# Steps of five tiles and a block of 128 nodes, with one-hots compared into PSUM and weighted from there

## The reference

```python
def _rgcn_conv(x, src, dst, et, basis, comp, root, bias):
    W = jnp.einsum('rb,bio->rio', comp, basis)
    xw = jnp.einsum('ni,rio->nro', x, W)
    msgs = xw[src, et]
    seg = dst * N_REL + et
    summed = jax.ops.segment_sum(msgs, seg, num_segments=N_NODES * N_REL)
    cnt = jax.ops.segment_sum(jnp.ones((msgs.shape[0],), x.dtype), seg, num_segments=N_NODES * N_REL)
    mean = summed / jnp.maximum(cnt, 1.0)[:, None]
    agg = mean.reshape(N_NODES, N_REL, HIDDEN).sum(axis=1)
    return agg + x @ root + bias
...
h = x
for l in range(N_LAYERS):
    h_new = jax.nn.relu(_rgcn_conv(h, src, dst, edge_type, basis[l], comp[l], root[l], bias[l]))
    h = h_new + h
...
out = _layernorm(x + h)
```

## Time and profile before

| | us |
|---|---|
| runs shown | 5449.66, 5447.10, 5457.17; median 5449.66 |
| the profiled execution, its own time | 5442.3 |
| its span | 5440.0 |
| granted TensorE clock over the span | 0.583 of full speed |
| PE busy | 2179.6 (40%) |
| DVE busy | 1661.3 (31%) |
| ACT busy | 1425.4 (26%) |
| POOL busy | 3015.8 (55%) |

### The profile page before, as it was taken

One profiled execution on the slowest core, in us unless ns is written; L12 is line 12 of the kernel. 1 busy time (PEld: TensorE's weight loads), 2 busy tenths in 40 slices (PEclk: granted clock), 3 DMA queues, 4 the chain that ended last, 5 costly groups with the idle time before them and its releaser, 6 DMA issues. The chain is left out here.

```text
span 5440.0 us, 53285 instructions
## 1 busy us (share of the span) xinstructions
PE 2179.6 (40%) x8413; PEld 1711.0 (31%) x8413; DVE 1661.3 (31%) x4647; ACT 1425.4 (26%) x4065; POOL 3015.8 (55%) x3194
## 2 busy tenths in 40 slices
PE   7823333333333333333496133333333333333336
PEld 4412232333223223233343133223333322333336
DVE  7402233233233233323320123223333323332336
ACT  5612222222222222222254022222222222222225
POOL 0355566665666656566303666666666665656652
PEclk9956555555555555555698555555555555555557
DMA  7711111111111111111054111111111111111113
GB/s 227 273 38 41 42 45 43 44 44 41 44 44 43 43 41 44 42 44 44 24 232 172 44 44 43 43 43 44 44 44 44 43 44 41 45 42 44 43 38 95
DMA packets 180986, 337.44 MB, mean 62 GB/s; under 512 B 64632, under 2 KB 104616, under 8 KB 180932
## 3 DMA queue, kind: packets, MB, share of 16 engines
q0 software_dynamic: 101488, 209.20, 14.7%
q1 hardware_dynamic: 53472, 114.78, 5.8%
q10 hardware_dynamic: 25972, 12.87, 0.9%
HBM read 225.40 MB, written 111.23 MB: 62 GB/s over the span
## 5 line engine op out<-in xcount | busy, mean ns | idle before, releaser
L332 POOL DMA_INDIRECT ring<-products,idx x3000 | 2830.1, 943 | 2037.9 <-issue 924.5
L713 PE MATMUL bank<-onehot,rows 128*128 128x128 f32 x6656 | 1668.7, 431 | 3086.5 <-DVE onehot L878 2439.6
L713 PEld LDWEIGHTS bank<-onehot,rows 128*128 128x128 f32 x6656 | 1438.6, 319 | 3316.8 <-DVE onehot L878 2467.4
L548 ACT ACTIVATE rows<-ring,relnorm 128x128 f32 x3328 | 1051.8, 389 | 3681.2 <-remote 2237.7
L888 DVE TENSOR_TENSOR aggT<-aggT,bank 128x128 f32 x3328 | 951.8, 286 | 1914.9 <-issue 1389.0
L878 DVE TENSOR_TENSOR onehot<-bank,relnorm 128x512 f32<-128x512 f32 x832 | 573.1, 689 | 1609.6 <-issue 1551.4
L623 PE MATMUL bank<-W,hT 128*128 128x512 f32 (+1 forms) x784 | 344.3, 598 | 12.5 <-ACT ring L503 7.2
L503 ACT ACTIVATE ring<-bank 128x512 f32<-128x512 f32 x392 | 233.2, 597 | 129.4 <-PE bank L623 112.6
L623 PEld LDWEIGHTS bank<-W,hT 128*128 128x128 f32 (+1 forms) x784 | 148.6, 192 | 194.0 <-issue 180.9
L332 POOL DMA_INDIRECT ring<-products,idx_rest x126 | 118.9, 944 | 73.1 <-issue 40.1
L610 PE MATMUL bank<-onehot,relnorm 128*128 128x128 f32 x256 | 50.7, 353 | 109.9 <-issue 99.8
(11 more groups left out here) (119 smaller groups left out, 433.0 us busy)
## 6 DMA issues: line engine op xcount, KB each, us to landing
products<-ring SPq DMA_DIRECT2D x194, 512.0 KB, 2.6
ring<-products,idx POOLq DMA_INDIRECT x3000
S<-x ACTq DMA_DIRECT2D x24, 256.0 KB, 4.5
onehot<-x ACTq DMA_DIRECT2D x24, 256.0 KB, 3.2
out<-S SPq DMA_DIRECT2D x24, 256.0 KB, 3.2
ring<-products,idx_rest POOLq DMA_INDIRECT x126
idx<-idxT SPq DMA_DIRECT2D x60, 25.0 KB
onehot<-basis SPq DMA_DIRECT2D x2, 512.0 KB, 6.1
```

The costliest lines, as they stand in the source:

```text
L332: g.indirect_dma_start(out=ring[0:R, slot * P:(slot + 1) * P], out_offset=None, in_=products[L.n], in_offset=bass.IndirectOffsetOnAxis(ap= ...
L548: s.activation(rows[0:R, u % 2 * BATCH + k, :], ring[0:R, bass.ds(v[2 * k + 1], P)], ACT.Copy, scale=relnorm[0:R, 1, bass.ds(b * BATCH + k ...
L713: last = t.matmul(bank[2 * (u % PB) + k // 4][:, k % 4 * P:(k % 4 + 1) * P], rows[0:R, at, :], onehot[0:R, at, :], start=True, stop=True)
```

## The change

A step is now a pack of five tiles (640 edges) and a window. There are 313 packs, 313 + 98 - 1 = 410 pairs, rounded up to 416 steps, in 52 turns of 8. In each step ScalarE copies the pack's five tiles out of the ring with one instruction of 640 columns, unscaled. VectorE makes five one-hots with one compare of 640 columns from PSUM into PSUM (`hot_psum`, over two banks), and multiplies them by the edges' weights into SBUF with a second instruction of 640 columns. TensorE makes five products that accumulate in one bank, and VectorE adds the bank once to the window's columns. There are four sets of one-hots, rows and banks (`HOTS`). All engines loop over turns, with one turn in the body and the first written out. VectorE's order is: match of step u, addition of step u - 1.

The gathers stay one to a tile, 1563 a layer. `FLIGHT` is 20 and `GROUP` is 10; SyncE frees slots by packs, counts `landed` in packs, and reads its table once for 50 tiles. The semaphores `scattered`, `added` and `onehots` start raised, so that their waits in a step have the same value. The tables follow: `relnorm` is 128 x 2 x 5 x 416, gathered in 4 groups of 128 steps with 640 numbers each, where there were 13 groups with 128 each, and turned in 16 parts. The host hands over the first and last destination of each pack in place of each tile.

```diff
-    BATCH = 8
-    BATCHES = -(-(TILES + WINDOWS - 1) // BATCH)
-    GROUPS = -(-BATCHES * BATCH // P)
+    PACK = 5
+    PACKS = -(-TILES // PACK)
...
+    TURN = 8
+    TURNS = -(-(PACKS + WINDOWS - 1) // TURN)
+    STEPS = TURNS * TURN
+    GROUPS = -(-STEPS // P)
     RING = 100
-    FLIGHT = 10
-    GROUP = 5
+    FLIGHT = 20
+    GROUP = 10
     LAG = RING - FLIGHT
...
-        relnorm = sb("relnorm", [P, 2, GROUPS * P])
+        relnorm = sb("relnorm", [P, 2, PACK, STEPS])
...
+        wide = ctx.enter_context(nc.psum_tensor("wide", [P, 2, 512], F32))
+        hot_psum = wide[:, :, :].rearrange("p b c -> p (b c)")[:, 0:PACK * P].rearrange("p (k c) -> p k c", k=PACK)
...
+        def over_turns(eng, body):
+
+            body(0)
+            with eng.Fori(1, TURNS) as i:
+                body(i)
...
+            def pass_on(L, block, landings, n, done):
+
+                if done is not None:
+                    sp.wait_ge(L.taken, done & COUNT_BITS)
+                    sp.nop(nofuse=True)
+                sp.wait_ge(L.got[block % 2], landings * (16 * GROUP) - 16 * (GROUP - n))
+                sp.sem_inc(L.landed, -(-n // PACK))
...
+            def take(L, i):
 
                 _, v = nc.values_load_multi_w_load_instructions(
...
+                for u in range(TURN):
+                    if u % 2 == 0:
+                        act.wait_ge(L.landed, v[2 * (u + 1)] & COUNT_BITS)
                         act.nop(nofuse=True)
-                        if late:
-                            act.wait_ge(L.scattered, 2 * (b - 2) + k // 4 + 1)
-                    s.activation(rows[0:R, u % 2 * BATCH + k, :], ring[0:R, bass.ds(v[2 * k + 1], P)], ACT.Copy,
-                                 scale=relnorm[0:R, 1, bass.ds(b * BATCH + k, 1)]).then_inc(L.weighted, 1)
+                        if not isinstance(i, int) or u >= HOTS:
+                            act.wait_ge(L.scattered, i * TURN + u + 3 - HOTS)
+                    s.activation(rows[0:R, u % HOTS * PACK:(u % HOTS + 1) * PACK, :].rearrange("p k c -> p (k c)"),
+                                 ring[0:R, bass.ds(v[2 * u + 1], PACK * P)], ACT.Copy).then_inc(L.taken, 1)
...
+            def scatter(L, i):
+
+                for u in range(TURN):
+                    pe.wait_ge(L.onehots, i * TURN + u + 2)
+                    pe.wait_ge(L.taken, i * TURN + u + 1)
+                    for k in range(PACK):
+                        at = u % HOTS * PACK + k
+                        last = t.matmul(bank[u % HOTS][:, 0:P], rows[0:R, at, :], onehot[0:R, at, :],
+                                        start=(k == 0), stop=(k == PACK - 1))
+                    last.then_inc(L.scattered, 1)
...
+            def match(L, i, u):
+
+                hot = onehot[0:R, u % HOTS * PACK:(u % HOTS + 1) * PACK, :]
+                of_turn = relnorm[0:R, :, :, bass.ds(i * TURN, TURN)]
+                keys = of_turn[:, 0, :, u:u + 1].to_broadcast([R, PACK, P])
+                weights = of_turn[:, 1, :, u:u + 1].to_broadcast([R, PACK, P])
+                dve.wait_ge(L.onehots, i * TURN + u + 1)
+                v.tensor_tensor(hot_psum, seg_psum[0:R].unsqueeze(1).to_broadcast([R, PACK, P]), keys,
+                                ALU.is_equal).then_inc(L.matched, 1)
+                dve.wait_ge(L.matched, i * TURN + u + 1)
+                v.tensor_tensor(hot, hot_psum, weights, ALU.mult).then_inc(L.onehots, 1)
+
+            def add_step(L, at, u, col):
+
+                dve.wait_ge(L.scattered, at + 1)
+                dve.wait_ge(L.added, at + 1)
                 to = aggT[:, bass.ds(col, WIN)]
-                v.tensor_tensor(to, to, bank[2 * (u % PB) + k // 4][:, k % 4 * P:(k % 4 + 1) * P],
-                                ALU.add).then_inc(L.added, 1)
+                v.tensor_tensor(to, to, bank[u % HOTS][:, 0:P], ALU.add).then_inc(L.added, 1)
```

More of the change, by code:

```diff
@@ L114, in build @@
         first_last = sb("first_last", [P, 4])
-        ends = rows[:, SPAN + 2, 0:2 * RELS]
-        bounds = rows[:, SPAN + 2, 2 * RELS:6 * RELS]
-        init = rows[:, SPAN + 2, 6 * RELS:8 * RELS]
+        ends = misc[:, SPAN + 2, 0:2 * RELS]
+        bounds = misc[:, SPAN + 2, 2 * RELS:6 * RELS]
+        init = misc[:, SPAN + 2, 6 * RELS:8 * RELS]
         NB = 8
@@ L203, in __init__ @@
                 self.onehots = sem(f"onehots_{n}")
-                self.weighted = sem(f"weighted_{n}")
+                self.matched = sem(f"matched_{n}")
+                self.taken = sem(f"taken_{n}")
                 self.scattered = sem(f"scattered_{n}")
@@ L263, in tiles_of, with steps_of @@
             return range(c * (CH // P), min(NODE_TILES, (c + 1) * (CH // P)))
+        def steps_of(g):
+            return min(P, STEPS - g * P)
+        table_parts = [(g, half, lo, hi) for g in range(GROUPS) for half in range(2) for lo, hi in ((0, 3), (3, PACK))]
         T_BANKS = ((4, 5, 6, 7), (0, 1, 2, 3, 4, 5))
@@ L437, in turn @@
+            def pass_on(L, block, landings, n, done):
[4 more added lines that the diff above has]
+                sp.sem_inc(L.landed, -(-n // PACK))
             def turn(L, t, reload=(True, True), first=False):
+                per_half, per_turn = HALF // GROUP, RING // GROUP
                 for half in range(2):
-                    for k in range(HALF // FLIGHT):
-                        at = half * HALF + k * FLIGHT
-                        landings = 16 * (t * (RING // FLIGHT) + (at // FLIGHT + 1))
-                        if first and at == LAG:
+                    for k in range(per_half):
+                        block = half * per_half + k
+                        if first and block * GROUP == LAG:
@@ L443, in turn @@
                             sp.wait_ge(tables_out, 48)
-                        pass_on(L, t * RING + at, FLIGHT, not first or at >= LAG, landings)
+                            done = done_by(0, per_turn - block)
+                        elif k == 0 and not first:
+                            done = done_by(t * (RING // PACK) + (half * HALF - LAG) // PACK, per_half)
+                        free = not first or block * GROUP >= LAG
+                        pass_on(L, block, t * (per_turn // 2) + block // 2 + 1, GROUP,
+                                done[block - LAG // GROUP if first else k] if free else None)
@@ L453, in _ @@
                 turn(L, ROUNDS - 1, reload=(False, False))
-                for i in range(0, REST, FLIGHT):
-                    pass_on(L, ROUNDS * RING + i, min(FLIGHT, REST - i), True, 16 * ((ROUNDS * RING + i) // FLIGHT + 1))
+                blocks = -(-REST // GROUP)
+                done = done_by((ROUNDS * RING - LAG) // PACK, blocks)
+                for k in range(blocks):
+                    pass_on(L, k, ROUNDS * (RING // GROUP // 2) + k // 2 + 1, min(GROUP, REST - k * GROUP), done[k])
                 if L.n == 0:
@@ L528, in _ @@
             keep_w(3)
-            for k in range(GROUPS):
-                act.wait_ge(table_turned, k + 1)
-                s.activation(relnorm[0:R, :, k * P:(k + 1) * P], bank[6 + k % 2][0:R, 0:2 * P].rearrange("p (t s) -> p t s", t=2),
+            for q, (g, half, lo, hi) in enumerate(table_parts):
+                act.wait_ge(table_turned, q + 1)
+                m = steps_of(g)
+                s.activation(relnorm[0:R, half, lo:hi, g * P:g * P + m],
+                             bank[6 + q % 2][0:R, 0:(hi - lo) * P].rearrange("p (k s) -> p k s", s=P)[:, :, 0:m],
                              ACT.Copy).then_inc(table_kept, 1)
@@ L881, in add_step @@
-            def add_step(L, b, u, k, col, first):
-                if k % 4 == 0:
-                    dve.wait_ge(L.scattered, 2 * b + k // 4 + 1)
-                if not first:
-                    dve.wait_ge(L.added, b * BATCH + k)
+            for L in layers:
+                dve.sem_inc(L.scattered, 1)
+                dve.sem_inc(L.added, 2)
+                dve.sem_inc(L.onehots, 1)
+            def match(L, i, u):
[8 more added lines that the diff above has]
+                v.tensor_tensor(hot, hot_psum, weights, ALU.mult).then_inc(L.onehots, 1)
@@ new lines, in body @@
+                def body(i):
+                    first = isinstance(i, int) and i == 0
+                    if first:
+                        dve.wait_ge(L.staged, 2 * NODE_TILES)
+                        match(L, i, 0)
+                        dve.wait_ge(L.agg_ready, CHUNKS)
+                        cols = columns(0, TURN - 1)
+                    else:
+                        cols = columns(i * TURN - 1, TURN)
+                    for u in range(first, TURN):
+                        match(L, i, u)
+                        add_step(L, i * TURN + u, (u - 1) % HOTS, cols[u - first])
@@ L917, in _ @@
+                over_turns(dve, body)
+                add_step(L, STEPS, (TURN - 1) % HOTS, columns(STEPS - 1, 1)[0])
+                dve.wait_ge(L.added, STEPS + 2)
                 for c in range(CHUNKS + 4):
@@ L933 @@
     full = src.shape[0] // rows * rows
```

(2 more changed lines are left out.)

187 lines of the change are left out of this document (70 added, 117 removed).

## The result

The changed kernel takes 5614.31 us (median of 4 runs, 5586.31 to 5626.47), the kernel before 5448.38 (median of 4, 5436.09 to 5457.17): a ratio of 1.0301, 95% interval 1.0277 to 1.0324. It is 3% slower. The forecast was 5260, the range 4900 to 5560; the time lies 54 us above its upper end. The profiled run took 5586.31, with a span of 5584.5 against 5440.0.

A forecast was written before the change was run, and what follows sets the result against it. Gathers wait on a full ring for the scatter, which slow stretches delay. From 5442.3 us: gathers -161 (1.530 to 1.475 us a tile), drain -27, preparation +3, 5257, say 5260; range 4900 to 5560.

The forecast's parts named there:

- slow stretch: Second half of a gather burst: register instructions end 0.70 us apart, 5.6 us a product; a tile 7.5 us against 6.0.
- drain: Scatter remaining after a layer's last gather: 90.6 us falls to 77, two times 13.5 saved.
- A fast turn: Eight scatter steps outside slow stretches, put at 22 us: 2.5 a step plus 0.29 for reading columns.
- q: Fast scatter time a gather burst leaves by itself: 6.8 us before; four readings gave 6.8, 8.7, 11.1 or 4.6 after.
- reading (b): VectorE's instruction count sets fast time: 4.7 a tile become 3.1, fast time 8.7 us, 1.475 us a tile; chosen.
- equation for a burst of 20: Scatter matches gathers per cycle: (q + s) / 0.74 + (24.96 - q) / 7.5 = 20 tiles.
- reading (d): Count of products sets fast time: 4.6 us, gap 8.2, 1.66 us a tile, 5800 us in all.
- the slower rival: Gather cycle costs more than before: 5503 us and up, decided from gaps of 5.8 us; chance 0.28.
- s: Gap in the gathers after a burst of 20, put at 4.5 us; over 5.8 would mean slower, under 2.5 faster.
- the burst of 20 with q not grown: Slower case in the gather cycle: fast time stays 6.8 us, gap 6.2, 1.56 us a tile, 5503 us.
- VectorE's loop code being loaded: Rival: slow stretches are code loads and vanish with the shorter loop, gathers at 1.248 us, 4590 us; chance 0.06.
- (c): Count over VectorE, ScalarE and SyncE sets fast time: 11.1 us, 1.36 us a tile, 4930 us; chance 0.18.

The follow-up runs named there:

- bfloat16: Changed kernel with copied messages and weighted one-hots written as bfloat16: 5263.9 us, 0.9634 of the kernel before.
- with its waits: Changed kernel with eight waits on VectorE behind each addition, on a semaphore reached long before: 5599.8 us, 1.0387 of the kernel before.
- four products: Changed kernel with four products a step instead of five, fifth tile's messages left out: 5466.1 us, 1.0074; on a fast chip 4432.3 us, 1.0065.
- half columns: Changed kernel with four of five products over 64 instead of 128 columns: 5624.7 us, 1.0371; on a fast chip 4438.8 us, 1.0078.
- of five with 20 in flight: Changed kernel with GROUP 5 instead of 10, FLIGHT still 20, four landing semaphores instead of two: 5379.1 us, 0.9975 of the kernel before.
- blocks of five: Changed kernel with GROUP 5 and FLIGHT 10 instead of 10 and 20: 5430.8 us, 1.0008; on a fast chip 4419.3 us, 1.0032.
- waits on GpSimd: Eight waits ahead of each gather: changed kernel with GROUP 5, FLIGHT 10, 5106.3 us, 0.9475; kernel before, no late products, 4403.2 us, 1.0000.
- Waits added on TensorE: Changed kernel with eight waits on TensorE behind each step's products, on a semaphore reached long before: 5609.4 us, 1.0338 of the kernel before.

## Why the prediction was wrong

**The bound.** It was right for the runs that it was made for: the ring is full, the gathers wait for the scatter, and a slow stretch ends most bursts, with 5.6 us a product at the longest. A step of five was put at 28 us in a slow stretch; the longest are 26.9. The 640-column instructions were put at 0.82 each and took 0.832 and 0.825. The drain was put at 77 and took 82.07.

**A fast turn.** It was put at 22 us. In the drain two turns' first compares stand 21.77 us apart, but not for the reasons given:

```profile
5457.62 0.83 DVE L907 TENSOR_TENSOR wide<-bank,relnorm 128x640 f32<-128x640 f32 x1 [5.07 <-issue]
...
5479.39 0.83 DVE L907 TENSOR_TENSOR wide<-bank,relnorm 128x640 f32<-128x640 f32 x1 [5.11 <-issue]
```

The read of eight columns takes 5.1 us, not the 2.33 of the earlier trace rows (its second load 3.7 us instead of 1.17), and the steps themselves 2.1 instead of 2.5, since products and one-hots overlap better than I let them. The two errors cancel, so the right total is luck.

**The value of q, the step that failed.** I chose reading (b), a count of VectorE's instructions, because VectorE and ScalarE were seen to crawl first, and let q grow from 6.8 to 8.7 us. The measured 1.584 us a tile, put into the prediction's own equation for a burst of 20, gives q = 6.2: it did not grow. The trace says the same of its own measure, the issue of the first late product after the gathers resume. Its median is 8.3 us in the changed kernel, 12.4 in the kernel before and 15.2 in bfloat16. How updates that the trace lacks (see the last section) and the smallest stops are treated moves these figures by up to 0.7 us, and that of bfloat16 by up to 2. This is not q itself, which was 6.8 for the kernel before, so only the direction and the ratio compare: down by a third, where I had it up.

VectorE's count does not set it (5600 us with its waits, and 9 us to the first late product). TensorE's load and product instructions, 5.3, 4.3 and 2.7 a tile in these three kernels, put them in the right order. This is reading (d) of the prediction, which I had left at the far end of the slower rival. It had q fall from 6.8 to 4.6, a factor of 0.68; the first late product moved from 12.4 to 8.3, 0.67. That the factors agree so well is luck, since the count alone does not fix this moment: four products and half columns, with 16 and 20 such instructions a step, both have it at some 9.5 us. What the count sets in those two runs is how long a late product takes (21.2 and 26.8 us at the longest). The rate of (d) was too high (1.66 us a tile against 1.584). One term of it was certainly too dear: it took every slow step at the full 28 us. Of the 609 steps measured 249 are over 1 us late, by 8.6 us on average; 28 is nearly the longest, not the usual one. What makes a product late at all stays open.

**The blocks of ten, the second term mis-sized.** I priced them inside the cycle by a gap of s = 4.5 us after a burst of 20. The stops are 6.0 us at the median, which is on the slower rival's side of the 5.8 that the prediction had named, and 7.6 on average, and bursts of 30 are nearly as frequent as those of 20. The rival "the burst of 20 with q not grown" named this mechanism and its sign; its price of 5503 was 111 us short. Undone by itself, the block size gives back the whole loss: the ratio to the kernel before goes from 1.0301 to 1.0008. The trace suggests why. In all three forms, blocks of ten, of five, and of five with 20 in flight, the first late product comes some 8.3 us after a resume, and the last one ends about 3 us after a stop. The good time that a resume gives is the same whatever the block, so it should matter how many there are: some 135, 195 and 175. The number alone is not the whole account, since the 175 go with a ratio of 0.9975, no worse than that of the 195. After the late step has ended, ten slots need two more steps and five need one.

**Steps of five tiles.** With blocks of five these stand alone and give 1.0008 (0.9990 to 1.0026), neither gain nor loss. The fifth product costs 121 to 151 us with blocks of ten. That VectorE and ScalarE save about as much as it costs follows by subtraction only; four products with blocks of five was not run.

**The other rivals.** If the stretches were VectorE's loop code being loaded, they would have vanished with the shorter loop (4590); they did not. The branch that the prediction reads at 0.40 us takes 0.34 from its end, which changes nothing. Fewer stretches by (c) (4930) falls too. The chance of slower, 0.28, was too small: two of the four readings of q were on that side, and I took the engine whose crawl I had looked at first.

## What to carry to other kernels

Where a producer is stopped by a full buffer, the size of the block that it waits for is a cost of its own: blocks of ten instead of five cost some 3% here, and asking for less at a time, or stopping the producer earlier than the full buffer does, gained more than halving two engines' instructions. Before a count of instructions is chosen as cause, separate the engines in the trace by who waits for whom: the engine that crawls visibly is not always the one that holds the others up. And run a pair on more than one chip before believing its per cents: the kernel before and the change with blocks of ten are 3% apart where products come late, and variants of that change within 0.8% of it where they do not.

## What the runs showed of the hardware that I had not expected

- The kernel before takes 4403 to 4405 us on two chips and 5392 to 5466 on three. Gathers take 943 to 944 ns in the traces of both kinds. What differs in the traces is slow stretches with late products, present or absent altogether. The cause is not settled, and chip and hour are not separated.
- Where products are late, the trace itself has holes: of 416 updates of `scattered` in layer 1 it holds 340 (before), 365 (changed) and 345 (four products); where none is late, 415 (the kernel before with waits on GpSimd) or all (blocks of five). The Trainium skill, "NOTIFIC — Programmer's Manual", section "When the ring fills", says that a queue of event records is set to one of three answers for when it is full: drop new records, overwrite the oldest, or stall the producer. Here records are missing and engines stand still in the same stretches, which no one of the three gives by itself. Still, part of the time may belong to the recording. Every run here was recorded, so this is a candidate and not shown.
- In a slow stretch the longest late products come to 1.33 to 1.43 us for each weight load and product instruction of the step, whatever its columns and type, and a register instruction or a wait takes 0.70. This is no fixed price: with the waits on GpSimd the longest is 12.5 us for the same 20 instructions, 0.63 each. Waits added on TensorE did not make its steps longer (26.8 us with them, 26.9 without).
- A `nop` put into the loops of TensorE and VectorE left no trace and no time; eight waits on a reached semaphore left four records a step, on either engine.
- Where no gather runs, the second load of the read of eight registers took 3.5 to 3.7 us from step 8i - 1 on, and 1.17 from step 8i on. The Trainium skill, "Runtime: NRT & Kernel Launch", section "Instruction fetch mechanics", gives some 200 ns a register. An estimate from that is 1.6 us for eight, which lies between the two measured times. Whether the start that is no multiple of eight is the reason was not tried.
